# Perceiver block on one core: latents and projection of the queries for two pairs in every second round, keys' rows by transposes, scores in two halves

## The chip, the cores and the metric

One core of one Trainium2 chip runs the whole program. The metric is device microseconds of one execution; the profile beside it is of one execution of its own, and all times in it count from the start of its span. TensorE is PE in the views, its weight loads PEld, VectorE is DVE, ScalarE is ACT, GpSimd is POOL, and SyncE (SP) issues the DMAs.

## The reference

There are 32 examples of 64 query tokens and 128 context tokens, 512 features each, all float32. Three residual blocks follow each other.

```python
# cross attention, 16 heads, latents of 32 (keys) and 64 (queries)
C_q = Q @ Wq_d ; C_kv = K @ Wkv_d            # Q = layernorm(x), K = ctx
CqWqk = (C_q @ W_qk).reshape(b, n, H, LKV)
scores = einsum('bnhl,bkl->bhnk', CqWqk, C_kv) / sqrt(LKV) ; attn = softmax(scores)
out = einsum('bhnk,bkhd->bnhd', attn, (C_kv @ Wv_u).reshape(b, nkv, H, HD))
# one-head self attention of width 128 on layernorm(x), with biases
# feed forward on layernorm(x): x @ hadamard, rows rounded to 4 bits, times ternary weights
```

## The kernel before, in words

Two examples make a pair: 128 query rows, 256 context rows; there are 16 pairs. All engines walk through rounds i = -1 to 17. Round i works on four pairs at once: `front` computes latents, projection and scores of pair i+1, `cross` the softmax and pooled values of pair i, `self_` the second attention of pair i-1, `quant` the feed forward of pair i-2. Rounds 4 to 11 are a hardware loop over two rounds (`par` = 0, then 1); the others are written out. The order in each engine's body is fixed by the code, and semaphores (`made`: written by TensorE, `read`: copied out of PSUM, `done`: by DVE, ACT or POOL) tie the engines. TensorE's queue is in order, so a wait in it holds up all behind it.

The steps that matter here, by lines of TensorE's body: L608 values of pair i-1 through Wv; L615 transposes of x3; L624 latents of the queries (weights 64 columns wide, two column halves of the array, each summing two chunks of features); L630 latents of the context (32 columns, four column strips); L644 Hadamard product; L649, L600, L683, L687 transposes and the q, k, v products of the second attention; L695 transposes of the rounded rows; L712 q times k; L656 projection of the query latents for all 16 heads (the two partial sums of L624 lie in 128 partitions, and `wqk2` holds W_qk twice, so the product adds them); L659 the context latents repeated in four strips (`ckv`, columns 0 to 255); L662 the same latents with the keys on partitions (`fold`, 32 columns each); L733 pooled values in latent space; L740 transpose of the second attention's probabilities p2; L753 ternary product (int); L758 o2t; L768 scores of the next pair, 32 products with 32 rows and 64 columns of weights, into banks 0 to 3; L778 output product of the second attention. A float32 product has two matmul records, a transpose one. PSUM has 8 banks: 0 to 3 for scores and transposed probabilities, B1 to B4 for all others.

ScalarE copies what TensorE made, between its exponentials: x3t, lat, x2t, prob_t, q_t, p2t, u_t, o2t. VectorE takes the maxima of the scores (L417), makes x3 (L540), sums, statistics and the rounding.

## Time and profile before

| | |
|---|---|
| median of 3 runs | 337.03 us (336.73 to 337.52) |
| the profiled execution, its own time | 338.82 us |
| its span | 337.0 us |
| TensorE busy | 318.1 us, 94% |
| VectorE, ScalarE, GpSimd busy | 239.7, 211.1, 88.2 us |
| mean share of the DMA engines in a round | 0.20 |

The profile has a page, and the trace behind it answers queries. In order of time a row gives start, duration, engine, line, what is written from what, how many records, and in brackets how long the engine had been idle and who ended it. The records of a matmul overlap, so that the start of the next row less the start of a row, not its duration, is what a step takes of TensorE's time.

### The profile page before, as it was taken

The numbers are of one execution on the slowest core, as the hardware profiler recorded it, in microseconds if no ns is written. First come the engines' busy times: TensorE is split into PE (matmuls) and PEld (weight loads), VectorE is DVE, ScalarE is ACT, GpSimd is POOL, SyncE is SP. The second block draws the span as 40 slices with busy tenths as digits, with TensorE's granted clock in tenths as the row PEclk, the third lists the DMA queues.
The fourth block names the chain that finished last, engine by engine and source line by source line (L and its number), as shares of the span: only waits on it lengthen the run. The fifth ranks groups of instructions, "written<-read, shape, count | busy, mean of one in ns | idle before, by whom it ended". The sixth has DMA issues, their size and how long they took to land.

```text
span 337.0 us, 8519 instructions
## 1 busy us (share of the span) xinstructions
PE 318.1 (94%) x3204; PEld 231.7 (69%) x3204; DVE 239.7 (71%) x517; ACT 211.1 (63%) x565; POOL 88.2 (26%) x129
## 2 busy tenths in 40 slices
PE   8897899999999999999999999999999999898995
PEld 6775666758595867768585857677685858575754
DVE  1489638686877868686868768686868778686435
ACT  2474858577586758586685867585866757673210
POOL 2000533131332323231223313232312223131320
PEclk9997999999999999999999999999999999999999
DMA  7891203040211303040402103030402020000000
GB/s 227 277 375 59 97 3 124 2 158 0 103 58 38 122 33 124 5 151 0 155 0 94 62 31 124 31 124 5 151 2 65 0 66 0 33 3 31 2 31 31
DMA packets 13481, 25.25 MB, mean 75 GB/s; under 512 B 3216, under 2 KB 3984, under 8 KB 13456
## 3 DMA queue, kind: packets, MB, share of 16 engines
q1 hardware_dynamic: 13456, 24.91, 21.0%
q8 instruction: 16, 0.26, 0.3%
q14 instruction: 9, 0.07, 0.1%
HBM read 20.71 MB, written 4.19 MB: 74 GB/s over the span
## 4 chain that ended last, share of the span: by engine, by line
PE 75%; DVE 15%; DMA 3%; ACT 2%; issue 2%; SPq 2%; DVEq 0%
PE ps L644 17%; PE ps L683 9%; PE ps L600 7%; DVE mx L417 6%; PE ps L768 5%; PE ps L733 5%; PE ps L656 5%; PE ps L687 4%; PE ps L753 4%; DVE x L540 3%; DMA w_rows<-weight 3%; PE ps L615 3%; PE ps L624 2%; PE ps L630 2%; PE ps L649 2%
## 5 line engine op out<-in xcount | busy, mean ns | idle before, releaser
L301 ACT ACTIVATE prob<-ps,nmx,qk_scale 128x128 f32<-128x128 f32 x256 | 95.9, 463 | 56.3 <-DVE nmx L421 56.3
L644 PE MATMUL ps<-had_s,x3t 128*128 128x512 f32 x128 | 59.2, 605 | 1.2 <-ACT x3t L295 1.2
L417 DVE TENSOR_REDUCE mx<-ps 128x8 f32<-128x1024 f32 x32 | 39.0, 1218 | 13.3 <-PE ps L768 13.3
L644 PEld LDWEIGHTS ps<-had_s,x3t 128*128 128x128 f32 x128 | 23.0, 189 | 30.1 <-issue 24.6
L426 DVE TENSOR_REDUCE sum_a<-prob 128x8 f32<-128x1024 f32 x32 | 37.5, 1209 | 2.3 <-ACT prob L301 2.3
L295 ACT ACTIVATE prob_t<-ps 128x512 f32<-128x512 f32 x64 | 35.1, 612 | 5.6 <-PE ps L600 5.5
L600 PE MATMUL ps<-ident,prob 128*128 128x128 f32 x256 | 33.3, 273 | 1.0 <-ACT prob L301 1.0
L288 POOL TENSOR_TENSOR res<-prod,x 128x512 f32<-128x512 f32 x15 | 19.0, 1267 | 57.0 <-DVE prod L530 57.0
L683 PE MATMUL ps<-x2t,wqkv_s 128*128 128x128 f32 x256 | 32.5, 280 | 0.8 <-ACT x2t L295 0.8
L683 PEld LDWEIGHTS ps<-x2t,wqkv_s 128*128 128x128 f32 x256 | 29.8, 191 | 2.0 <-ACT x2t L295 1.2
L284 POOL TENSOR_TENSOR qk_scale<-aux,power 128x1 f32<-128x1 f32 x16 | 8.8, 548 | 83.1 <-DVE aux L496 83.1
L600 PEld LDWEIGHTS ps<-ident,prob 128*128 128x128 f32 x256 | 28.3, 141 | 1.7 <-ACT prob L301 1.5
L262 POOL TENSOR_TENSOR rstd<-aux,power 128x1 f32<-128x1 f32 x16 | 8.8, 548 | 69.7 <-DVE aux L446 69.7
L530 DVE SCALAR_TENSOR_TENSOR prod<-ps,qscale,scale_row 128x512 f32<-128x512 f32 x15 | 11.3, 751 | 19.0 <-PE ps L753 19.0
L608 PEld LDWEIGHTS ps<-wv_bd,u_t 128*128 128x128 f32 x128 | 17.3, 197 | 7.2 <-issue 7.2
L279 POOL TENSOR_TENSOR x2b<-x,const_row 128x512 f32<-128x512 f32 x16 | 20.3, 1270 | 0.1
L768 PE MATMUL ps<-ckv,q_t 32*64 32x128 f32 x1024 | 19.3, 278 | 0.1
L656 PE MATMUL ps<-lat,wqk 128*128 128x128 f32 x128 | 18.4, 287 | 0.2 <-ACT lat L295 0.2
L778 PE MATMUL ps<-wo_s,o2t 128*128 128x512 f32 x32 | 18.0, 645 | 0.5 <-ACT o2t L295 0.4
L733 PE MATMUL ps<-prob_t,ckv 128*32 128x256 f32 x256 | 17.1, 383 | 0.9 <-ACT prob_t L295 0.5
L608 PE MATMUL ps<-wv_bd,u_t 128*128 128x128 f32 x128 | 17.6, 282 | 0.0
L768 PEld LDWEIGHTS ps<-ckv,q_t 32*64 32x64 f32 x1024 | 15.5, 130 | 2.4 <-issue 0.7
(114 smaller groups left out, 566.0 us busy)
## 6 DMA issues: line engine op xcount, KB each, us to landing
ct<-ctx_cols SPq DMA_DIRECT2D x16, 512.0 KB, 3.7
xt<-x_cols SPq DMA_DIRECT2D x16, 256.0 KB, 2.6
xr<-x_rows SPq DMA_DIRECT2D x16, 256.0 KB, 3.8
y<-res SPq DMA_DIRECT2D x15, 256.0 KB, 2.0
w_rows<-weight SPq DMA_DIRECT2D x1, 1024.0 KB, 10.5
had_s<-hadamard SPq DMA_DIRECT2D x1, 1024.0 KB, 8.6
wqkv_s<-wqkv SPq DMA_DIRECT2D x1, 768.0 KB, 10.2
wqk<-w_qk SPq DMA_DIRECT2D x2, 128.0 KB, 4.1
```

Source lines behind the costliest of these rows:

```text
L279: nc.gpsimd.tensor_tensor(x2b[:], x2[:], const_row[:], ALU.add).then_inc(done["x2b"], 1)
L295: return nc.scalar.activation(dst, src, ACT.Copy)
L301: last = nc.scalar.activation(prob[:, h, :], ps[:, h // 4, (h % 4) * P:(h % 4) * P + P], ACT.Exp, bias=nmx[:, h:h + 1], scale=qk_scale[:])
L417: V.tensor_reduce(mx[:, h], ps[:, 2 * half:2 * half + 2, :].rearrange("p r (c k) -> p (r c) k", c=EC), AX.X, ALU.max).then_inc(done["mx"], 1)
L426: V.tensor_reduce(sum_a[:, h], prob[:, h, :], AX.X, ALU.add).then_inc(done["sum"], 1)
L600: mm = pe.transpose(ps[:, r, c * P:(c + 1) * P], prob[:, 4 * r + c, :], ident[:])
L608: mm = pe.matmul(ps[:, B1, c * P:(c + 1) * P], u_t[:, c, :], wv_bd[:, c, :], start=True, stop=True)
L644: mm = pe.matmul(ps[:, B4, :], x3t[:, c, :], had_s[:, c, :], start=(c == 0), stop=(c == EC - 1))
L656: mm = pe.matmul(ps[:, B2, c * P:(c + 1) * P], wqk2[:, c * P:(c + 1) * P], lat[:, 0:P], start=True, stop=True)
L683: mm = pe.matmul(ps[:, B1, s * P:(s + 1) * P], wqkv_s[:, c, s * P:(s + 1) * P], x2t[:, c, :], start=(c == 0), stop=(c == EC - 1))
L733: mm = pe.matmul(ps[32 * r:32 * r + 32, B2, :].rearrange("p (c t) -> p c t", c=EC) [:, :, 64 * bb:64 * bb + 64], ckv[:, par, 2 * SKV + LAT ...
L768: mm = pe.matmul(ps[64 * bb:64 * bb + 64, r, c * P:(c + 1) * P], q_t[g, bb, c, :], ckv[g, 1 - par, bb * SKV:(bb + 1) * SKV], start=True, s ...
```

## The change

The latents of the queries and their projection are made for two pairs at once, in the odd rounds (`par == 1`); even rounds have neither, but for rounds -1 and 0, which do one pair each as before (`alone`). In an odd round the query latents come right behind L608's step: the two column halves of the array take a pair each, all four chunks of features are summed in place, so `lat` holds pair i+1 in partitions 0 to 63 and pair i+2 in 64 to 127. The projection then multiplies 64 rows of each, alternating between the halves of partitions, into bank 0 and bank 1, behind the v product; ScalarE copies the two banks to two slots of `q_t`. Even rounds copy only the context's columns of `lat`.

The keys' rows are no longer products with `fold`: at the next round's head two transposes of `ckv` go to bank B3, and ScalarE copies 32 columns of each to `ckv_k`. The latents move from B3 to B2, x3's transposes from B2 to B4. The transpose of p2 comes behind the int product, and the scores are cut in two halves, one ahead of o2t and one behind it. On VectorE the maximum of the second attention moves ahead of the row statistics of the next pair. SyncE loads x for two pairs in odd rounds.

```diff
         lat = sb("lat", [P, P + 2 * SKV])
-        q_t = sb("q_t", [P, 2, EC, SQ])
-        ckv = sb("ckv", [P, 2, 2 * SKV + 2 * LAT])
+        q_t = sb("q_t", [P, 2, 2, EC, SQ])
+        ckv = sb("ckv", [P, 2, 2 * SKV])
+        ckv_k = sb("ckv_k", [P, 2, LAT])
...
         def _(sp):
-            def load_cols(pair, par):
-                after(sp, made["lat"], pair - 2)
+            def load_queries(pair, par):
                 sp.dma_start(xt[:, par], x_cols[bass.ds(pair, 1)].rearrange("o p c t -> (o p) c t")).then_inc(ld_xt[par], 16)
+            def load_context(pair, par):
...
             sp.dma_start(wqkv_s[:], wqkv.rearrange("(c p) n -> p c n", p=P)).then_inc(ld_w["wqkv"], 16)
-            load_cols(2, 0)
+            sp.wait_ge(made["lat"], 1)
+            load_queries(2, 0)
+            load_context(2, 0)
...
                 if not pre or 0 <= i < PAIRS - 3:
-                    load_cols(i + 3, 1 - par)
+                    after(sp, made["lat"], i + 1)
+                    if pre and i == 0:
+                        load_queries(i + 3, 1)
+                    elif par == 1:
+                        load_queries(i + 3, 0)
+                        if not pre or i + 4 < PAIRS:
+                            load_queries(i + 4, 1)
+                    load_context(i + 3, 1 - par)
...
+                def q_copy(slot, bank):
+                    copy(q_t[:, slot], ps[:, bank, :].rearrange("p (c b q) -> p b c q", c=EC, b=2)).then_inc(read["qt"], 1)
...
                     after(act, made["had"], i - 3)
-                    copy(x3t[:], ps[:, B2, :].rearrange("p (c t) -> p c t", c=EC)).then_inc(read["x3t"], 1)
+                    copy(x3t[:], ps[:, B4, :].rearrange("p (c t) -> p c t", c=EC)).then_inc(read["x3t"], 1)
...
                     after(act, made["lat"], i + 1)
-                    copy(lat[:], ps[:, B3, 0:P + 2 * SKV]).then_inc(read["lat"], 1)
+                    cols = slice(0 if alone(i) or par == 1 else P, P + 2 * SKV)
+                    copy(lat[:, cols], ps[:, B2, cols]).then_inc(read["lat"], 1)
+                if cross:
+                    after(act, made["ckvk"], i)
+                    after(act, made["u"], i - 1)
+                    copy(ckv_k[:], ps[:, B3, 0:2 * P].rearrange("p (b l) -> p b l", b=2)[:, :, 0:LAT])\
+                        .then_inc(read["ckvk"], 1)
...
                     copy(v2[:], ps[:, B2, 0:P]).then_inc(read["v"], 1)
+                if front and par == 1 and not alone(i):
+                    act.wait_ge(made["qt"], k + 3)
+                    q_copy(0, 0)
...
                     pt_copy(3)
-                if front:
+                if front and alone(i):
                     after(act, made["qt"], i + 1)
-                    copy(q_t[:], ps[:, B2, :].rearrange("p (c b q) -> p b c q", c=EC, b=2)).then_inc(read["qt"], 1)
+                    q_copy(1 - par, query_bank(i))
+                elif front and par == 1:
+                    q_copy(1, 1)
...
                     after(act, made["ckv"], i + 1)
-                    copy(ckv[:, 1 - par], ps[:, B1, 0:2 * SKV + 2 * LAT]).then_inc(read["ckv"], 1)
+                    copy(ckv[:, 1 - par], ps[:, B1, 0:2 * SKV]).then_inc(read["ckv"], 1)
...
                         .then_inc(read["qit"], 1)
+                if self_:
+                    after(dve, made["s2"], i - 1)
+                    V.tensor_reduce(mx2[:], ps[:, B3, 0:SQ], AX.X, ALU.max).then_inc(done["mx2"], 1)
+                    after(dve, done["mx2"], i - 1)
+                    V.tensor_scalar(nmx2[:], mx2[:], -float(D2) ** -0.5, None, ALU.mult).then_inc(done["nmx2"], 1)
...
                     mm.then_inc(made["xo"], 1)
+                if front and alone(i):
+                    pe.wait_ge(ld_xt[1 - par], 16)
+                    for h in range(2):
+                        for t in range(2):
+                            c = 2 * t + h
+                            pe.matmul(ps[64 * t:64 * t + 64, B2, 0:P], wq_c[:, c, :], xt[:, 1 - par, c, :],
+                                      start=(h == 0), stop=(h == 1))
+                elif front and par == 1:
+                    for t in range(2):
+                        pe.wait_ge(ld_xt[t], (k + 2) * 16)
+                    for c in range(EC):
+                        for t in range(2):
+                            pe.matmul(ps[64 * t:64 * t + 64, B2, 0:P], wq_c[:, c, :], xt[:, t, c, :],
+                                      start=(c == 0), stop=(c == EC - 1))
...
                     after(pe, read["wo"], i - 2)
-                    for c in range(EC):
-                        mm = pe.transpose(ps[:, B2, c * P:(c + 1) * P], x3[:, par, c * P:(c + 1) * P], ident[:])
+                    after(pe, read["int"], i - 3)
+                    if first and i == 2:
+                        pe.wait_ge(row_read, 1)
+                    for c in range(EC):
+                        mm = pe.transpose(ps[:, B4, c * P:(c + 1) * P], x3[:, par, c * P:(c + 1) * P], ident[:])
...
                 if front:
-                    if first and i == 1:
-                        pe.wait_ge(ternt_read, 2)
-                    pe.wait_ge(ld_xt[1 - par], (k + par + 1) * 16)
-                    for h in range(2):
-                        for t in range(2):
-                            c = 2 * t + h
-                            pe.matmul(ps[64 * t:64 * t + 64, B3, 0:P], wq_c[:, c, :], xt[:, 1 - par, c, :],
-                                      start=(h == 0), stop=(h == 1))
...
                     for c in range(EC):
-                        mm = pe.matmul(ps[32 * c:32 * c + 32, B3, P:P + 2 * SKV], wkv_s[:, c, :], ct[:, 1 - par, c, :],
+                        mm = pe.matmul(ps[32 * c:32 * c + 32, B2, P:P + 2 * SKV], wkv_s[:, c, :], ct[:, 1 - par, c, :],
...
                     mm.then_inc(made["lat"], 1)
+                if cross:
+                    after(pe, read["ckv"], i)
+                    if quant:
+                        after(pe, read["wo"], i - 2)
+                    if first and i == 1:
+                        pe.wait_ge(ternt_read, 2)
+                    for bb in range(2):
+                        mm = pe.transpose(ps[:, B3, bb * P:(bb + 1) * P], ckv[:, par, bb * SKV:(bb + 1) * SKV], ident[:])
+                    mm.then_inc(made["ckvk"], 1)
...
                     after(pe, read["x3t"], i - 2)
-                    after(pe, read["int"], i - 3)
                     if first and i == 2:
-                        pe.wait_ge(row_read, 1)
...
                     after(pe, done["x2n"], i - 1)
+                    if front:
+                        after(pe, read["lat"], i + 1)
...
                     mm.then_inc(made["x2t"], 1)
+                def scores(half):
+                    for c in (2 * half, 2 * half + 1):
+                        for r in range(4):
+                            g = slice(32 * r, 32 * r + 32)
+                            for bb in range(2):
+                                mm = pe.matmul(ps[64 * bb:64 * bb + 64, r, c * P:(c + 1) * P], q_t[g, 1 - par, bb, c, :],
+                                               ckv[g, 1 - par, bb * SKV:(bb + 1) * SKV], start=True, stop=True)
+                    return mm
...
                         pe.wait_ge(fold_made, 2)
-                    for c in range(EC):
-                        mm = pe.matmul(ps[:, B2, c * P:(c + 1) * P], wqk2[:, c * P:(c + 1) * P], lat[:, 0:P],
-                                       start=True, stop=True)
-                    mm.then_inc(made["qt"], 1)
+                    if alone(i):
+                        for c in range(EC):
+                            mm = pe.matmul(ps[:, query_bank(i), c * P:(c + 1) * P], wqk2[:, c * P:(c + 1) * P], lat[:, 0:P],
+                                           start=True, stop=True)
+                        mm.then_inc(made["qt"], 1)
                     pe.matmul(ps[:, B1, 0:2 * SKV], fold4[:].rearrange("p r l -> p (r l)"), lat[:, P:P + 2 * SKV],
-                              start=True, stop=True)
-                    for bb in range(2):
-                        mm = pe.matmul(ps[:, B1, 2 * SKV + LAT * bb:2 * SKV + LAT * (bb + 1)],
-                                       lat[:, P + SKV * bb:P + SKV * (bb + 1)], fold[:], start=True, stop=True)
-                    mm.then_inc(made["ckv"], 1)
+                              start=True, stop=True).then_inc(made["ckv"], 1)
...
                     mm.then_inc(made["v"], 1)
+                if front and par == 1 and not alone(i):
+                    pe.wait_ge(read["pt"], i * 4 + 2)
+                    for c in range(EC):
+                        for t in range(2):
+                            g = slice(64 * t, 64 * t + 64)
+                            mm = pe.matmul(ps[:, t, c * P:(c + 1) * P], wqk2[g, c * P:(c + 1) * P], lat[g, 0:P],
+                                           start=True, stop=True)
+                    mm.then_inc(made["qt"], 1)
...
                     after(pe, read["qk"], i - 1)
-                    if front:
-                        after(pe, read["lat"], i + 1)
+                    if cross:
+                        after(pe, read["ckvk"], i)
...
                     after(pe, read["lat"], i + 1)
-                    if self_:
-                        after(pe, read["v"], i - 1)
...
                     if first and i == -1:
-                        keep_busy(2, 0)
+                        keep_busy(2, B3)
...
                     pe.wait_ge(read["pt"], i * 4 + 4)
-                    if front:
-                        after(pe, read["qt"], i + 1)
-                    elif self_:
+                    after(pe, read["ckvk"], i)
+                    if first and i == 0:
+                        pe.wait_ge(read["qt"], 2)
+                    if self_:
...
                                            [:, :, 64 * bb:64 * bb + 64],
-                                           ckv[:, par, 2 * SKV + LAT * bb:2 * SKV + LAT * (bb + 1)],
+                                           ckv_k[:, bb, :],
...
                     mm.then_inc(made["u"], 1)
-                if self_:
-                    after(pe, done["exp2"], i - 1, 2)
-                    pe.transpose(ps[:, B3, 0:P], p2[:], ident[:]).then_inc(made["p2t"], 1)
...
                 if self_:
+                    after(pe, done["exp2"], i - 1, 2)
+                    pe.transpose(ps[:, B3, 0:P], p2[:], ident[:]).then_inc(made["p2t"], 1)
+                if front:
+                    if alone(i):
+                        after(pe, read["qt"], i + 1)
+                    elif par == 1:
+                        pe.wait_ge(read["qt"], 2 * k + 4)
+                    after(pe, read["ckv"], i + 1)
+                    if cross:
+                        pe.wait_ge(read["pt"], i * 4 + 4)
+                    scores(0)
+                if self_:
...
                 if front:
-                    after(pe, read["qt"], i + 1)
-                    after(pe, read["ckv"], i + 1)
-                    if cross:
-                        pe.wait_ge(read["pt"], i * 4 + 4)
-                    for c in range(EC):
-                        for r in range(4):
-                            g = slice(32 * r, 32 * r + 32)
-                            for bb in range(2):
-                                mm = pe.matmul(ps[64 * bb:64 * bb + 64, r, c * P:(c + 1) * P], q_t[g, bb, c, :],
-                                               ckv[g, 1 - par, bb * SKV:(bb + 1) * SKV], start=True, stop=True)
-                    mm.then_inc(made["s"], 1)
+                    scores(1).then_inc(made["s"], 1)
```

The order of TensorE's instructions in the second round of the loop body (the odd one) at its head, before and then of the change; L608 and L641 are the same step, as are L615 and L665, L630 and L672, L644 and L693.

```order
L608 MATMUL ps<-wv_bd,u_t 128x128 x4
L615 MATMUL ps<-ident,x 128x128 x4
L620 ISA
L624 MATMUL ps<-xt,wq_c 64x128 x4
L630 MATMUL ps<-ct,wkv_s 32x256 x4
L644 MATMUL ps<-had_s,x3t 128x512 x4
```

```order
L641 MATMUL ps<-wv_bd,u_t 128x128 x4
L652 ISA
L655 MATMUL ps<-xt,wq_c 64x128 x8
L665 MATMUL ps<-ident,x 128x128 x4
L672 MATMUL ps<-ct,wkv_s 32x256 x4
L682 MATMUL ps<-ident,ckv 128x128 x2
L693 MATMUL ps<-had_s,x3t 128x512 x4
```

The query latents have moved ahead of x3's transposes, eight products instead of four, and two transposes of ckv stand ahead of the Hadamard product. The even round has the same rows without L652 and L655.

The order of TensorE's instructions at the end of the same round, from q times k on, before and then of the change; L656 and L752 are the projection, L733 and L797 the pooled values, L768 and L707 the scores.

```order
L712 MATMUL ps<-k,q 64x64 x2
L656 MATMUL ps<-lat,wqk 128x128 x4
L659 MATMUL ps<-lat,fold 128x256
L662 MATMUL ps<-fold,lat 128x32 x2
L726 ISA
L733 MATMUL ps<-prob_t,ckv 32x4x64 x8
L740 MATMUL ps<-ident,p 128x128
L753 MATMUL ps<-tern_t,qi_t 128x512 x4
L758 MATMUL ps<-p2t,v 128x128
L768 MATMUL ps<-ckv,q_t 64x128 x32
L778 MATMUL ps<-wo_s,o2t 128x512
```

```order
L777 MATMUL ps<-k,q 64x64 x2
L720 MATMUL ps<-lat,fold 128x256
L789 REGISTER_ALU
L797 MATMUL ps<-prob_t,ckv_k 32x4x64 x8
L814 MATMUL ps<-tern_t,qi_t 128x512 x4
L818 MATMUL ps<-ident,p 128x128
L823 REGISTER_ALU
L707 MATMUL ps<-ckv,q_t 64x128 x16
L831 MATMUL ps<-p2t,v 128x128
L707 MATMUL ps<-ckv,q_t 64x128 x16
L841 MATMUL ps<-wo_s,o2t 128x512
```

The products with `fold` of 32 columns are gone, the projection has left this place, the int product is ahead of the transpose of p2, and o2t stands between the halves of the scores.

The projection's new place, in TensorE's order of the change, odd round, between the v product and the transposes of the rounded rows:

```order
L740 MATMUL ps<-x2t,wqkv_s 128x128 x8
L744 MATMUL ps<-wqkv_s,x2t 128x128 x4
L748 ISA
L752 MATMUL ps<-lat,wqk 128x128 x8
L760 MATMUL ps<-ident_b,qi 128x128 x4
```

Before, these rows stood there without L748 and L752.

## Rows read from the trace of the kernel before

**Rows 1.** The page, part 1: busy time, share of the span, instructions.

```profile
PE 318.1 (94%) x3204; PEld 231.7 (69%) x3204; DVE 239.7 (71%) x517; ACT 211.1 (63%) x565; POOL 88.2 (26%) x129
```

**Rows 2.** Whom TensorE waited for: us in total, times, longest.

```profile
PE ps L615 <- DVE x L540: 5.7, 15, 0.8
...
PE ps L649 <- POOL x2n L265: 0.6, 1, 0.6
```

**Rows 3.** Busy time of each engine in one round, clock, DMA share, GB/s.

```profile
162.10:180.68 18.58, 18.25 (x192) 13.23 (x192) 14.40 (x32) 13.03 (x37) 5.16 (x7) 1.00 0.20 69
```

**Rows 4.** TensorE in order of time, one round of the loop.

```profile
171.67 1.04 PE L600 MATMUL ps<-ident,prob 128*128 128x128 f32 x8
172.64 0.34 PE L712 MATMUL ps<-k,q 128*64 128x64 f32 x4
172.91 1.16 PE L656 MATMUL ps<-lat,wqk 128*128 128x128 f32 x8
173.90 0.60 PE L659 MATMUL ps<-lat,fold 128*128 128x256 f32 x2
174.34 0.53 PE L662 MATMUL ps<-fold,lat 128*128 128x32 f32 x4
174.84 1.07 PE L733 MATMUL ps<-prob_t,ckv 128*32 128x256 f32 x16
175.84 0.33 PE L740 MATMUL ps<-ident,p 128*128 128x128 f32 x1
176.01 1.03 PE L753 MATMUL ps<-tern_t,qi_t 128*128 128x512 bf16 x4
176.87 0.38 PE L758 MATMUL ps<-p2t,v 128*128 128x128 f32 x2
177.19 1.21 PE L768 MATMUL ps<-ckv,q_t 32*64 32x128 f32 x64
178.32 1.12 PE L778 MATMUL ps<-wo_s,o2t 128*128 128x512 f32 x2
179.29 1.05 PE L608 MATMUL ps<-wv_bd,u_t 128*128 128x128 f32 x8
180.68 0.66 PE L615 MATMUL ps<-ident,x 128*128 128x128 f32 x4 [0.33 <-DVE x L540]
181.26 0.66 PE L624 MATMUL ps<-xt,wq_c 128*64 128x128 f32 x8
181.85 0.64 PE L630 MATMUL ps<-ct,wkv_s 128*32 128x256 f32 x8
182.42 3.70 PE L644 MATMUL ps<-had_s,x3t 128*128 128x512 f32 x8
```

**Rows 5.** All engines in order of time, the next round; rows of DVE, ACT, PE.

```profile
179.87 0.75 DVE L540 SCALAR_TENSOR_TENSOR x<-ps,rsum,x2b 128x512 f32<-128x512 f32 x1
...
181.37 0.60 ACT L295 ACTIVATE x3t<-ps 128x512 f32<-128x512 f32 x1
...
190.89 1.09 ACT L295 ACTIVATE prob_t<-ps 128x512 f32<-128x512 f32 x2 [0.39 <-PE ps L600]
...
193.18 0.30 ACT L354 ACTIVATE p<-ps,nmx 64x64 f32<-64x64 f32 x1
...
194.43 0.33 PE L740 MATMUL ps<-ident,p 128*128 128x128 f32 x1
...
194.79 0.28 ACT L295 ACTIVATE p2t<-ps 128x128 f32<-128x128 f32 x1 [0.34 <-PE ps L740]
...
195.45 0.38 PE L758 MATMUL ps<-p2t,v 128*128 128x128 f32 x2
...
195.87 0.28 ACT L295 ACTIVATE o2t<-ps 128x128 f32<-128x128 f32 x1 [0.32 <-PE ps L758]
```

**Rows 6.** TensorE in order of time, round 15.

```profile
304.82 0.33 PE L740 MATMUL ps<-ident,p 128*128 128x128 f32 x1
...
306.60 1.13 PE L778 MATMUL ps<-wo_s,o2t 128*128 128x512 f32 x2 [0.37 <-ACT o2t L295]
```

**Rows 7.** TensorE in order of time, end of round 0.

```profile
26.97 1.05 PE L589 MATMUL ps<-ident_b,tern 128*128 128x128 bf16 x16 [2.08 <-DVE const_row L454]
```

21 lines of the change are left out of this document (11 added, 10 removed).

## The prediction

> **What bounds the kernel now.** I read the page's first part, then who TensorE waited for, then one round of the loop in order of time on TensorE, then the same round on the other engines, last the ends of the program. TensorE is busy 94% of the span [rows 1]. A round of the loop takes 18.58 us, TensorE is busy 18.25 of it, at a granted clock of 1.00 [rows 3]. The rest is one wait: L615, the transposes of x3, waits 0.33 us for DVE's x3 in each round (5.7 us in 15 rounds, the longest item of its waits) [rows 2, 4]. VectorE (14.40) and ScalarE (13.03) have 4 and 5 us to spare per round [rows 3]. So a microsecond of TensorE's time taken from a round is a microsecond of the kernel, as long as the copies on ScalarE between two of its steps still arrive in time. The reader should see in [rows 4] that the next start less this start is the price of a step, and that this price has two parts: a full-array record of 128 columns costs 0.11 us (L600: 8 in 0.97, which at a change of shape holds 0.1 more), however few columns it streams (L662: 4 records of 32 columns in 0.50); and where the shape of the weights changes, the step before pays about 0.1 us more (L758: 2 records in 0.32). Steps in narrow tiles overlap: L768 has 64 records in 1.13 us, over 4 row strips times 2 column halves, 8 records per tile; L624 has 4 per tile in 0.59 [rows 4]. From these two a block of narrow tiles costs 0.59 for 4 records per tile and 1.0 to 1.1 for 8.
>
> **The change, part by part, in us of TensorE's time.** Even rounds project nothing; odd rounds do two pairs.
> (A) L656, L659, L662 filled 172.91 to 174.84, 1.93 us [rows 4]. L656 leaves this place and L662 goes. What stays is one product of two 256-column records before a change of shape; the nearest step is L630 with two 256-column records per tile, 0.57 [rows 4]; its weights are narrower, so I add half a 0.11 us record: 0.62. Each round: -1.31.
> (B) L624 goes: -0.59 [rows 4].
> (C) Two transposes of ckv are put ahead of the Hadamard product: 2 x 0.11, less a weight load that is now hidden under them: +0.19.
> (D) The end of the round, L733 to L778, took 174.84 to 178.32, 3.48 us [rows 4]. The int product is now ahead of the transpose of p2, and the scores stand in two halves around o2t. New: pooled values 1.03, int product 0.86 + 0.05 (first weight load bare), transpose 0.11 + 0.1 (before a tiled step), half the scores 0.62 (4 records per tile: between L624's 0.59 and 0.65), o2t 0.42 (L758's 0.32 and a bare weight load), half the scores 0.62; together 3.82: +0.34. If the split were free it would be 0; if each half cost what the whole costs, +1.4. I take the rate by records per tile.
> (E) Odd rounds: the latents of two pairs, 8 records per tile, stand between L608's step and x3's transposes: 1.02, and the change of shape 0.2. L608 start to L615 start was 1.39 with the 0.33 wait in it [rows 4]; now 0.98 + 1.02 = 2.00, and x3 (179.87 + 0.75 [rows 5]) is there long before: +0.61.
> (F) Odd rounds: the projection of two pairs in 16 records, K = 64 each, into two banks. No row shows a 64-row strip. If the two strips overlap as L768's four do, it is 8 records per strip at 0.11, entry 0.2, exit 0.2, a bare load 0.1 and 0.05 behind it, less what the neighbour gave up: +1.23. If the strips do not overlap, 16 x 0.11 + 0.35 = 2.1. I take 1.23, since L768 proves overlap between row strips: without it 64 records over two column halves would be 32 x 0.11 = 3.5 us, not 1.13.
> Even round: -1.31 - 0.59 + 0.19 + 0.34 = -1.37. Odd round: the same + 0.61 + 1.23 = +0.47.
>
> **Who could be late.** Measured from the step that each waits for: x3t's copy starts 0.69 after L615 (181.37 against 180.68) and takes 0.60, so the Hadamard product may start at 1.34; its turn comes at 0.58 + 0.57 + 0.22 = 1.37 now, 1.74 before [rows 4, 5]. Tight, no wait. The last prob_t copies end at 191.98, 0.76 behind the start of q.k at 191.22 (172.64 a round earlier [rows 4]); the pooled values' turn is now at 0.27 + 0.62 = 0.89. Tight too. Softmax 2's exponentials (193.18) no longer sit behind the q_t copy: DVE's maximum is moved ahead of the row statistics, and they are done 1 us before the transpose needs them. Behind that maximum on DVE are only the row statistics of the next pair, needed 3 us later. p2t is copied 0.36 after L740's start, for 0.28 [rows 5]; the first half of the scores covers 0.8. o2t's copy ends 0.70 behind L758's start (195.87 + 0.28 against 195.45), behind u_t's on ScalarE; its cover is 0.42 + 0.62. In odd rounds the first q_t copy fits between v's and prob_t's. The ckv_k copy (some 0.25) falls into ScalarE's wait for DVE's second nmx. If a cover fails, each costs 0.1 to 0.3 per round, 1.5 to 4 us in all. The x loads for two pairs are issued two rounds ahead; with DMA at 0.20 [rows 3] and landings of a few us that is hidden.
>
> **The ends.** At the start nothing is won: the ternary weights' transposes wait 2.08 for DVE [rows 7], and in round 1 TensorE waits 0.6 for x2n [rows 2], which swallows the longer latents. Round 1 itself gives 0.3. Rounds 15 and 16 have no scores to cover the p2t copy: from L740 to L778 took 1.78 [rows 6]; now 0.91 (int) + 0.31 + 0.28 + 0.05 (copy, laid bare) + 0.53 + 0.28 + 0.05 = 2.41, so +0.63 each, +1.3 together.
>
> **Sum.** Rounds 2 to 13 are six even and six odd: 6 x (-0.90) = -5.4; round 14 (even) -1.4; round 1 -0.3; the end +1.3. Together -5.8. The profiled execution took 338.82 (span 337.0), so 333.0; the median of the runs is 337.03, 1.8 below it, so **331.2**.
>
> **A rule weighed.** L662's 32-column records cost 0.11 to 0.125 us each [rows 4]. The Trainium skill (TensorEngine Tiling (Array Packing), Instruction Overhead) says that a matmul has about 60 cycles of overhead, so that fewer columns than that save nothing; by it the four records would cost about 0.1 us together, and removing them would give 6 us less than I count over 16 rounds. The trace decides: 0.50.
>
> **Rivals.**
> (1) The strips take turns in (F) because a strip cannot load weights while it streams: 2.1 instead of 1.23 in 7 rounds, +6.1, 337.3: no change. For it: no 64-row row exists. Against: L768's records, 8 per tile in 1.13, leave 0.11 per record and no room for a bare 64-column load each. The Trainium skill (TensorE: Matmul & The Clock Gate, The mechanism) says that a weight load overlaps with a running matmul only where the row group differs; by that rule this rival is the forecast, but full-array records come here every 0.11 us, each with a weight load of its own [rows 4], so the trace disagrees. Chance 0.08.
> (2) Slower: the strips write all 128 columns of the array, and each record waits for the other strip's end, as at a change of shape (0.2 instead of 0.11): 16 x 0.2 + 0.35 = 3.5, +16 us in 7 rounds, 347. The point is 2.06 per projection: above it the change loses. Chance 0.06.
> (3) The covers fail: o2t's or p2t's copy, or x3t's and prob_t's, stalls TensorE 0.1 to 0.3 in most rounds: 332.7 to 335.5. For it: four margins of 0.03 to 0.3. Against: each is worked out from copies that are in the rows. Chance 0.18.
> (4) The change of shapes costs less than I take it for, and (D) is near zero: -0.3 x 13, 327.5 to 329.5. Chance 0.08.
> (5) The forecast, 329.5 to 332.7: chance 0.60.
>
> **Numbers.** The range 329.3 to 335.0 holds (5), most of (3) and some of (4). 0.2% (0.7 us) is about what a measurement of this kernel tells from no change: faster 0.86, same 0.07, slower 0.07.
>
> **What the profile after would show.** Odd and even rounds of about 19.05 and 17.2 us in turn. The projection as 16 records of 64*128 in 1.1 us, not 2; the two halves of the scores 0.62 each; the 0.33 wait for x3 only in even rounds; TensorE's waits for x3t, prob_t, p2t, o2t still near zero in the loop, and 0.3 to 0.4 at p2t in rounds 15 and 16. Wrong would be: projection records 0.1 us apart, or a new wait of over 0.1 us per round on one of the four copies.

## The result, and the profile after

| | before | the change |
|---|---|---|
| median of the runs made side by side | 337.27 us (336.73 to 337.85, 4 runs) | 331.31 us (331.07 to 331.48, 4 runs) |
| ratio | | 0.9823, 95% interval 0.9803 to 0.9842 |
| the profiled execution, its own time; span | 338.82; 337.0 us | 331.07; 329.3 us |

The change is faster by 6.0 us, 0.1 from the forecast of 331.2. That total hides two errors that nearly cancel (rounds 2 to 14 gained 0.4 us less than forecast, the end lost 0.4 less), so that the last tenth is luck; and the experiments found an order of the same work that is about 5 us better still.

The page of the change, part 1, answers to [rows 1]: TensorE is still the engine that is nearly always busy, with 6.9 us less work.

```profile
PE 311.2 (95%) x3157; PEld 216.7 (66%) x3172; DVE 239.8 (73%) x517; ACT 210.6 (64%) x581; POOL 88.3 (27%) x129
```

Whom TensorE waited for in the change (us in total, times, longest); it answers to [rows 2]. The wait for x3 is left in 9 rounds of the 15, and its sum fell from 5.7 to 4.0. The row with "issue" is not a wait: of the four records of L814 the first is missing in the trace, so that the gap ahead of the other three looks idle.

```profile
PE ps L665 <- DVE x L573: 4.0, 9, 0.6
PE ps L814 <- issue: 2.2, 14, 0.2
...
PE ps L740 <- ACT x2t L314: 0.8, 2, 0.5
PE ps L831 <- ACT p2t L314: 0.7, 2, 0.4
```

Two rounds of the loop in the windows view, the even one and then the odd one (span, then busy time of PE, PEld, DVE, ACT, POOL, granted clock, DMA share, GB/s); they answer to [rows 3]. Both together take 36.50 us, where two rounds of before take 2 x 18.58 = 37.16.

```profile
155.13:172.68 17.55, 16.91 (x181) 11.30 (x174) 14.35 (x31) 12.34 (x35) 5.08 (x8) 1.00 0.18 60
172.68:191.63 18.95, 18.79 (x212) 13.10 (x205) 14.49 (x31) 13.52 (x37) 5.25 (x8) 1.00 0.27 83
```

TensorE in order of time over these two rounds; it answers to [rows 4]. L841 opens a round.

```profile
155.13 1.12 PE L841 MATMUL ps<-wo_s,o2t 128*128 128x512 f32 x2
...
157.63 0.65 PE L665 MATMUL ps<-ident,x 128*128 128x128 f32 x4 [0.48 <-DVE x L573]
158.21 0.64 PE L672 MATMUL ps<-ct,wkv_s 128*32 128x256 f32 x8
...
159.06 3.69 PE L693 MATMUL ps<-had_s,x3t 128*128 128x512 f32 x8
...
163.02 1.04 PE L633 MATMUL ps<-ident,prob 128*128 128x128 f32 x8
164.06 2.05 PE L740 MATMUL ps<-x2t,wqkv_s 128*128 128x128 f32 x16
...
168.31 0.70 PE L720 MATMUL ps<-lat,fold 128*128 128x256 f32 x2
168.94 1.07 PE L797 MATMUL ps<-prob_t,ckv_k 128*32 128x256 f32 x16
170.16 0.81 PE L814 MATMUL ps<-tern_t,qi_t 128*128 128x512 bf16 x3 [0.16 <-issue]
...
171.01 0.69 PE L707 MATMUL ps<-ckv,q_t 32*64 32x128 f32 x32
171.64 0.49 PE L831 MATMUL ps<-p2t,v 128*128 128x128 f32 x2
172.06 0.69 PE L707 MATMUL ps<-ckv,q_t 32*64 32x128 f32 x32
172.68 1.13 PE L841 MATMUL ps<-wo_s,o2t 128*128 128x512 f32 x2
...
174.62 1.09 PE L655 MATMUL ps<-xt,wq_c 128*64 128x128 f32 x16
175.65 0.66 PE L665 MATMUL ps<-ident,x 128*128 128x128 f32 x4
...
180.97 1.04 PE L633 MATMUL ps<-ident,prob 128*128 128x128 f32 x8
181.84 2.03 PE L740 MATMUL ps<-x2t,wqkv_s 128*128 128x128 f32 x16
183.71 1.06 PE L744 MATMUL ps<-wqkv_s,x2t 128*128 128x128 f32 x8
184.70 1.16 PE L752 MATMUL ps<-lat,wqk 64*128 64x128 f32 x16
185.79 0.40 PE L760 MATMUL ps<-ident_b,qi 128*128 128x128 bf16 x4
```

Start to next start gives the prices: the products with `fold4` 168.94 - 168.31 = 0.63; the latents of two pairs 1.03; the projection of two pairs 185.79 - 184.70 = 1.09; a half of the scores 0.63 (171.64 - 171.01), o2t between them 0.42.

### The profile page after: what moved, and what is told of

It is laid out like the page before. It is cut to its first block, busy times and chain, and to the rows that moved or that the text cites. A ratio compares the mean times of both kernels' runs of the same rounds, so it can differ in the third digit from the quotient of the medians.

```text
span 329.3 us, 8506 instructions
## 1 busy us (share of the span) xinstructions
PE 311.2 (95%) x3157; PEld 216.7 (66%) x3172; DVE 239.8 (73%) x517; ACT 210.6 (64%) x581; POOL 88.3 (27%) x129
## 4 chain that ended last, share of the span: by engine, by line
PE 79%; DVE 11%; DMA 3%; issue 2%; ACT 2%; SPq 2%; DVEq 0%
PE ps L693 17%; PE ps L740 9%; PE ps L633 8%; PE ps L707 6%; PE ps L797 5%; PE ps L744 4%; PE ps L814 4%; DVE mx L450 4%; PE ps L665 3%; PE ps L720 3%; PE ps L841 3%; DMA w_rows<-weight 3%; PE ps L752 2%; PE ps L672 2%; PE ps L831 2%
## 5 line engine op out<-in xcount | busy, mean ns | idle before, releaser
L693 PE MATMUL ps<-had_s,x3t 128*128 128x512 f32 x128 | 58.4, 599 | 0.9 <-ACT x3t L314 0.9
L693 PEld LDWEIGHTS ps<-had_s,x3t 128*128 128x128 f32 x128 | 23.0, 189 | 24.8 <-issue 23.0
L633 PE MATMUL ps<-ident,prob 128*128 128x128 f32 x256 | 33.4, 274 | 0.8 <-ACT prob L320 0.8
L740 PE MATMUL ps<-x2t,wqkv_s 128*128 128x128 f32 x256 | 32.7, 281 | 0.8 <-ACT x2t L314 0.8
L740 PEld LDWEIGHTS ps<-x2t,wqkv_s 128*128 128x128 f32 x256 | 29.8, 191 | 2.9 <-ACT x2t L314 2.2
L633 PEld LDWEIGHTS ps<-ident,prob 128*128 128x128 f32 x256 | 28.2, 141 | 2.0 <-ACT prob L320 1.8
L707 PE MATMUL ps<-ckv,q_t 32*64 32x128 f32 x1024 | 21.8, 280 | 0.2 <-ACT ckv L314 0.2
L641 PEld LDWEIGHTS ps<-wv_bd,u_t 128*128 128x128 f32 x128 | 16.7, 192 | 7.2 <-issue 7.2
L707 PEld LDWEIGHTS ps<-ckv,q_t 32*64 32x64 f32 x1024 | 14.6, 131 | 6.1 <-issue 4.0
L841 PE MATMUL ps<-wo_s,o2t 128*128 128x512 f32 x32 | 18.0, 645 | 0.5 <-ACT o2t L314 0.4
L797 PE MATMUL ps<-prob_t,ckv_k 128*32 128x256 f32 x256 | 17.1, 385 | 1.0 <-ACT q_t L314 0.5
L582 PE MATMUL ps<-mean_w 128*128 128x128 f32 x102 | 15.8, 298 | 1.4 <-POOL p L261 1.4
L641 PE MATMUL ps<-wv_bd,u_t 128*128 128x128 f32 x128 | 16.9, 275 | 0.0
```

What stands on the lines that cost most here:

```text
L633: mm = pe.transpose(ps[:, r, c * P:(c + 1) * P], prob[:, 4 * r + c, :], ident[:])
L641: mm = pe.matmul(ps[:, B1, c * P:(c + 1) * P], u_t[:, c, :], wv_bd[:, c, :], start=True, stop=True)
L693: mm = pe.matmul(ps[:, B4, :], x3t[:, c, :], had_s[:, c, :], start=(c == 0), stop=(c == EC - 1))
L707: mm = pe.matmul(ps[64 * bb:64 * bb + 64, r, c * P:(c + 1) * P], q_t[g, 1 - par, bb, c, :], ckv[g, 1 - par, bb * SKV:(bb + 1) * SKV], star ...
L740: mm = pe.matmul(ps[:, B1, s * P:(s + 1) * P], wqkv_s[:, c, s * P:(s + 1) * P], x2t[:, c, :], start=(c == 0), stop=(c == EC - 1))
L797: mm = pe.matmul(ps[32 * r:32 * r + 32, B2, :].rearrange("p (c t) -> p c t", c=EC) [:, :, 64 * bb:64 * bb + 64], ckv_k[:, bb, :], prob_t[: ...
```

## The experiments

Beside the experiments the kernel before was measured again on three chips, with medians of 337.99, 338.04 and 337.85 where it had 337.27 beside the change, so kernels are compared by their ratio to it, and a difference of ratios is turned into us with 338. "Even, odd" are loop rounds from output product to output product; the change has 17.54 and 18.95 to 18.96.

| kernel | median us | ratio, 95% interval | even, odd |
|---|---|---|---|
| the change | 331.31 | 0.9823, 0.9803 to 0.9842 | 17.54, 18.95 |
| e1_strip_order | 335.14 | 0.9926, 0.9897 to 0.9955 | 17.55, 19.50 |
| e2_scores_whole | 335.72 | 0.9932, 0.9911 to 0.9953 | 17.80, 19.29 |
| e4_keys_by_products | 337.38 | 0.9987, 0.9968 to 1.0006 | 17.91, 19.32 |
| e5_one_pair | 341.28 | 1.0102, 1.0069 to 1.0134 | 18.95, 18.73 |
| e9_one_pair_bank0 | 333.55 | 0.9864, 0.9838 to 0.9889 | 18.44, 18.21 |
| e3_old_end | 327.49 | 0.9684, 0.9662 to 0.9705 | 17.26, 18.79 |
| e6_unrolled | 330.41 | 0.9769, 0.9746 to 0.9792 | 17.34, 18.96 |
| e7_old_end_copy_late | 327.0 | 0.9668, 0.9646 to 0.9690 | 17.26, 18.69 |
| e8_old_end_unrolled | 326.17 | 0.9651, 0.9625 to 0.9677 | 17.02, 18.69 |
| e10_old_end_max_late | 335.72 | 0.9939, 0.9916 to 0.9962 | 18.34, 18.90 |
| e11_max_late | 334.38 | 0.9893, 0.9867 to 0.9919 | 18.01, 18.96 |

**The order of the strips.** The projection does one half of the partitions first and then the other.

```diff
-                    for c in range(EC):
-                        for t in range(2):
+                    for t in range(2):
+                        for c in range(EC):
                             g = slice(64 * t, 64 * t + 64)
```

> The changed kernel with one edit: the 16 records of the projection in odd rounds go through all four column groups of the first 64-row strip, then all four of the second, instead of alternating. Theory: the strips overlap only where neighbouring records go to different strips, so the block takes 16 x 0.11 + 0.25 = 2.0 us instead of 1.09; +0.9 in 7 rounds, +6.3 us, about 337.6. Rival: TensorE's queue looks far enough ahead to overlap the strips in any order, 331.3 unchanged. The price of the first rival of the prediction (strips take turns) is thereby measured too.

TensorE in order of time, the projection in an odd round of this kernel:

```profile
187.01 1.71 PE L752 MATMUL ps<-lat,wqk 64*128 64x128 f32 x16
188.66 0.40 PE L760 MATMUL ps<-ident_b,qi 128*128 128x128 bf16 x4
```

The block takes 1.65 us, against 1.09, and the odd round 0.55 more; 7 such rounds are 3.85 us, and the ratios differ by 1.0% (3.5 us). So neither theory had it. Taken one by one, the records of a strip start 0.112 us apart in either order, from its second record on. Alternated, the records of the two strips start in pairs, 0.006 apart. In sequence the second strip's first record starts at 187.57, just behind the fifth of the first strip's eight, so that only the last three of the first strip run beside the second: most of the overlap is lost, but not all. The two strips also write two banks, 0 and 1, in both orders; which of the two differences lets them overlap, rows or banks, no run separates.

**Scores in one piece behind o2t**, the transpose of p2 still behind the int product.

```diff
+                if self_:
+                    after(pe, read["p2t"], i - 1)
+                    after(pe, read["v"], i - 1)
+                    pe.matmul(ps[:, B3, 0:P], v2[:], p2t[:], start=True, stop=True).then_inc(made["o2t"], 1)
                 if front:
...
                     scores(0)
-                if self_:
-                    after(pe, read["p2t"], i - 1)
-                    after(pe, read["v"], i - 1)
-                    pe.matmul(ps[:, B3, 0:P], v2[:], p2t[:], start=True, stop=True).then_inc(made["o2t"], 1)
-                if front:
                     scores(1).then_inc(made["s"], 1)
```

> The changed kernel with one edit: all scores stand behind o2t in one block, as before, the transpose of p2 stays behind the int product. Theory: the first half of the scores covers the p2t copy, which is laid bare now: from the transpose's start 0.27 + 0.04 + 0.28 + 0.05 = 0.64 to o2t, 0.42 for o2t, 1.14 for the scores, 2.2 us against 1.87 now; +0.33 in 14 rounds, +4.6 us, about 336. Rival: the split costs more (two changes of shape) than it covers, and undoing it gives 0.1 to 0.2 per round, 328.5 to 330.

TensorE in this kernel, the end of a round:

```profile
175.90 0.49 PE L822 MATMUL ps<-p2t,v 128*128 128x128 f32 x2 [0.37 <-ACT p2t L314]
```

The theory held: the copy of p2t is laid bare in every round, 0.37 us, as in rounds 15 and 16 of the change, and an odd round is 0.34 longer, an even one 0.26. (With the scores in one piece VectorE's maximum starts 0.11 behind the start of the output product, with two halves 0.18, and only the even round, which waits for x3, gains by that.) The split pays once the transpose stands where it does. Whether the transpose should stand there is the next question but one.

**The keys' rows by products with `fold` again**, 32 columns each, and the transposes of ckv and the ckv_k copy gone.

```diff
-                    for bb in range(2):
-                        mm = pe.transpose(ps[:, B3, bb * P:(bb + 1) * P], ckv[:, par, bb * SKV:(bb + 1) * SKV], ident[:])
-                    mm.then_inc(made["ckvk"], 1)
...
+                    for bb in range(2):
+                        mm = pe.matmul(ps[:, B1, 2 * SKV + LAT * bb:2 * SKV + LAT * (bb + 1)],
+                                       lat[:, P + SKV * bb:P + SKV * (bb + 1)], fold[:], start=True, stop=True)
```

> The changed kernel with the keys' rows made as before, by two 32-column products with fold behind the repeated latents; the two transposes of ckv and the copy ckv_k are gone. Theory: the products cost 0.31 to 0.4 per round (L659 to L733 took 0.94 before, the same place takes 0.63 now), and taking the transposes (0.28) out from ahead of the Hadamard product gives nothing back, since x3t's copy ends there at the same moment: +0.31 to 0.4 in 15 rounds, 336 to 337.3. Rival: the transposes cost their own 0.28 of TensorE's time, so undoing is worth 0.03 to 0.1 per round: 331.8 to 332.8.

TensorE in this kernel: the head of the round, and the products' place.

```profile
162.97 0.64 PE L667 MATMUL ps<-ct,wkv_s 128*32 128x256 f32 x8
163.80 3.70 PE L679 MATMUL ps<-had_s,x3t 128*128 128x512 f32 x8 [0.20 <-ACT x3t L314]
...
173.07 0.70 PE L706 MATMUL ps<-lat,fold 128*128 128x256 f32 x2
...
174.06 1.07 PE L788 MATMUL ps<-prob_t,ckv 128*32 128x256 f32 x16
```

The transposes are nearly free: where they stood, TensorE now waits 0.20 for x3t. L672 to L693 was 0.85 in the change and L667 to L679 is 0.83 here, so that removing them gives 0.02 back, while the block at L706 costs 0.99 instead of 0.63. 0.36 in each of 15 rounds is 5.4 us, the ratios differ by 1.64%, 5.5 us. Without this part nearly the whole gain is gone; what it would be worth by itself, with the other parts undone, no run shows.

**One pair per round.** Latents and projection of one pair in each round, as in the kernel before, with the rest of the change kept; the projection goes to bank B2.

```diff
         def alone(i):
-            return isinstance(i, int) and i <= 0
+            return True
...
+                    if front:
+                        after(pe, read["qt"], i + 1)
```

> The changed kernel with latents and projection of one pair in every round, the latents still ahead of x3's transposes and in the new banks, keys by transposes and scores in halves kept. Theory: even rounds gain the projection's 0.89, the latents' 0.59 lie in the place of the 0.48 wait for x3 and take the 0.17 wait for x2t away: +0.76; odd rounds lose 1.18 (paired projection), 0.44 (second pair's latents) and gain 0.89: -0.73. Together about 0, 331 to 333: pairing itself is worth next to nothing against one pair a round at the new place. Rival: pairing is where the gain is; 1.78 - 1.18 = 0.6 per two rounds and more lost again, 335.5 or above.

Whom TensorE waited for in this kernel, the first row; and one such wait in order of time:

```profile
PE ps L794 <- ACT q_t L309: 6.9, 15, 0.5
```

```profile
155.21 1.16 PE L712 MATMUL ps<-lat,wqk 128*128 128x128 f32 x8
156.21 0.60 PE L715 MATMUL ps<-lat,fold 128*128 128x256 f32 x2
157.25 1.07 PE L794 MATMUL ps<-prob_t,ckv_k 128*32 128x256 f32 x16 [0.45 <-ACT q_t L309]
```

This missed by 8 to 10 us, and the miss teaches more than the hits. The pooled values write the bank that the q_t copy reads. In the kernel before L659 and L662 covered this copy for 0.94 us [rows 4]; with L662 gone only 0.59 is left, and each round waits 0.45. The wait makes 6.9 us of the miss. To test that, the same kernel with the projection in bank 0, which the pooled values don't write:

```diff
                     if alone(i):
+                        if self_:
+                            pe.wait_ge(read["pt"], i * 4 + 1)
                         for c in range(EC):
```

> As the kernel with one pair a round, but the projection is written to bank 0 (free once the first prob_t copy is done) instead of B2, so that the pooled values, which overwrite B2, no longer wait for the q_t copy. In the run before that wait took 0.45 us in each of 15 rounds, 6.9 us, and was not in my sum. Theory: without it a pair of rounds takes 36.8 to 36.9 against 36.5, so about +2.5 us on the change, 333 to 335: most of what pairing is worth is this wait, not TensorE's work. Rival: TensorE's work for one pair a round is itself worth more than 1 us per two rounds, and this is still at 338 or above.

The wait is gone, the ratio is 0.9864, and its two rounds take 18.44 + 18.21 = 36.65 us, where the change takes 36.50. So in the loop two pairs at once are in themselves worth 0.15 us per two rounds. Over the whole kernel the ratios differ by 0.4%, 1.4 us, with intervals that just overlap; by the two profiles 1.5 us of the change's lead arise in rounds 12 to 14. What pairs bought was mainly room: banks 0 and 1 for the projection, away from the tight copy. Bank 0 alone buys nearly the same.

**The kernel before once more**, for its start.

> The kernel before, looked at once more, for its start. In the profile of before the ternary weights' transposes (L589) start at 26.97 us, in that of the change at 25.28, while the medians differ by 6.0 and the spans by 7.7. Theory: the weight matrix landed late by chance (10.5 us against 8.5), and this look at before shows L589 at 25 to 26 or another value again. Rival: the change's start is 1.7 us shorter by its own doing, and before shows 26.9 again.

```profile
27.78 1.07 PE L589 MATMUL ps<-ident_b,tern 128*128 128x128 bf16 x16
```

This row is that of [rows 7]: 27.78 here, 26.97 there, and L622, the same step, at 25.28 in the change. The loop's rounds are the same 18.58 in both executions of before. The step started at another moment again, but not because of the weight matrix: w_rows landed in 8.0 us here and 10.5 there, and the 2.08 us wait of [rows 7] is absent; TensorE was later all along (the scores of round 0, L768, at 26.64 against 23.69). In the eight experiments that leave the change's start as it is, L622 starts at 24.79 to 27.96 and the transposes of x2n in round 1 at 33.77 to 36.43; in the two executions of before these stand at 35.95 and 36.17, in the change at 34.00. So the start moves by 2.7 to 3.2 us between executions, for a reason that stays open, and the 1.95 us by which the change's profile leads at that step is not shown to be the change's doing. It is why the spans differ by 7.7 us where the rest of the program accounts for 5.75.

The profile of before has one more thing at its start. TensorE stood idle for 2.08 us up to 26.97, and its granted clock was 0.56 from 28 to 29 us, 0.50 from 29 to 31 and 0.73 from 31 to 32: for most of this time it ran at 1.2 GHz instead of 2.4, and L608's step took 1.75 us where it takes about 1.0 in the loop. The other execution of before had no such idle time there and a clock of 1.00 in the same stretches; yet the two reach the output product of round 1 at 48.10 and 48.32, since x2n ends a wait in both (0.62 and 0.89 us) that takes most of it up.

**The order of before at the round's end**: transpose of p2, int product, o2t, scores in one piece.

```diff
                     mm.then_inc(made["u"], 1)
+                if self_:
+                    after(pe, done["exp2"], i - 1, 2)
+                    pe.transpose(ps[:, B3, 0:P], p2[:], ident[:]).then_inc(made["p2t"], 1)
                 if quant:
...
                 if self_:
-                    after(pe, done["exp2"], i - 1, 2)
-                    pe.transpose(ps[:, B3, 0:P], p2[:], ident[:]).then_inc(made["p2t"], 1)
+                    after(pe, read["p2t"], i - 1)
+                    after(pe, read["v"], i - 1)
+                    pe.matmul(ps[:, B3, 0:P], v2[:], p2t[:], start=True, stop=True).then_inc(made["o2t"], 1)
...
```

The step of o2t between the halves of the scores goes, as in e2_scores_whole.

> The changed kernel with the end of the round in the order of before: transpose of p2, int product, o2t, all scores in one block. Theory: the order of before took 3.48 us from the pooled values on, the new one takes 3.74, and p2's exponentials are done 0.1 us before their new turn in even rounds and 0.1 to 0.15 behind it in odd ones: -0.26 in 7 even rounds, -0.13 in 7 odd ones, -2.7 us and the 0.6 of rounds 15 and 16: about 328. Rival: without the projection and the fold products between q.k and the pooled values the exponentials are late by more than 0.3 us per round, and the new order was needed: 331 or above.

The median is 327.49 for a forecast of about 328, and the ratio falls to 0.9684, 4.7 us under the change. So the new order of the end is a loss that the rest of the change pays for. In a second step the second q_t copy of odd rounds goes behind the exponentials of the second attention and the ckv copy on ScalarE:

```diff
-                elif front and par == 1:
-                    q_copy(1, 1)
...
                     copy(ckv[:, 1 - par], ps[:, B1, 0:2 * SKV]).then_inc(read["ckv"], 1)
+                    if par == 1 and not alone(i):
+                        q_copy(1, 1)
```

> As the kernel with the old end of the round, and ScalarE's second q_t copy of odd rounds moved behind p2's exponentials and the ckv copy. Theory: it takes 0.6 us out of the way of the exponentials, so odd rounds gain the full 0.26 as well; it is 0.9 us less than the run before, about 327.2. Rival: the copy is then late for the scores, and it is not faster than the run before.

TensorE at the end of a round of this kernel:

```profile
168.53 1.07 PE L797 MATMUL ps<-prob_t,ckv_k 128*32 128x256 f32 x16
169.58 0.33 PE L804 MATMUL ps<-ident,p 128*128 128x128 f32 x1
...
170.61 0.39 PE L822 MATMUL ps<-p2t,v 128*128 128x128 f32 x2
170.92 1.21 PE L707 MATMUL ps<-ckv,q_t 32*64 32x128 f32 x64
172.06 1.13 PE L840 MATMUL ps<-wo_s,o2t 128*128 128x512 f32 x2
```

From the pooled values to the output product it takes 172.06 - 168.53 = 3.53 us, the change 3.74; the int product again covers the p2t copy, the scores in one piece the o2t copy, and the odd round is 0.1 shorter than in e3_old_end, though the medians of the two don't differ by more than their intervals.

**The maximum of the second attention late.** VectorE takes it behind the row statistics again, as in the kernel before, first in e7 and then in the change itself.

```diff
-                if self_:
-                    after(dve, made["s2"], i - 1)
-                    V.tensor_reduce(mx2[:], ps[:, B3, 0:SQ], AX.X, ALU.max).then_inc(done["mx2"], 1)
...
                     V.tensor_scalar(aux1[:], mv1[:, 1:2], EPS, float(LAT), ALU.add, ALU.mult).then_inc(done["aux1"], 1)
+                if self_:
+                    after(dve, made["s2"], i - 1)
+                    V.tensor_reduce(mx2[:], ps[:, B3, 0:SQ], AX.X, ALU.max).then_inc(done["mx2"], 1)
...
```

> As the kernel with the old end and the late copy, with VectorE's maximum of the second attention behind the row statistics of the next pair again, as in the kernel before. Theory: in even rounds the exponentials of p2 come 1.0 to 1.1 us later (0.68 + 0.2 + 0.2 of statistics), and the transpose of p2, which has no slack there, waits as long: +0.9 in 7 even rounds, nothing in odd ones, where the statistics are done before q.k: about 333.5 where that kernel is 327. Rival: the order on VectorE is free, 327.

> The changed kernel with one edit, VectorE's maximum of the second attention behind the row statistics again. Theory: the exponentials are done 0.7 us before their turn now, and would be 0.4 late in even rounds: +0.4 x 7 = +2.8, about 334. Rival: the new place of the transpose, behind the int product, has slack enough, 331.3 unchanged; then the move on VectorE buys nothing in the change as it stands.

All engines in order of time in e10_old_end_max_late, the rows of the second attention:

```profile
170.73 0.34 PE L777 MATMUL ps<-k,q 128*64 128x64 f32 x4
...
172.43 0.22 DVE L532 TENSOR_REDUCE mx<-ps 128x1 f32<-128x64 f32 x1
...
173.75 0.33 PE L804 MATMUL ps<-ident,p 128*128 128x128 f32 x1 [1.05 <-ACT p L385]
```

The first kernel missed its forecast of 333.5 by 2 us: its even rounds are 1.08 longer than in e7_old_end_copy_late, for 0.9, and its odd rounds 0.21, for nothing. The second came out as forecast. The scores of the second attention are there at 171.07 (170.73 + 0.34), VectorE comes to them at 172.43, and TensorE waits 1.05. The two lines on VectorE are worth 9 us with the old end (0.9668 against 0.9939) and 2.4 us in the change (0.9823 against 0.9893), where the int product ahead of the transpose covers part of the lateness. In the kernel before, the projection and the products with `fold` stood between these scores and the transpose: L712 to L740 took 3.20 us [rows 4], L777 to L804 takes 1.97 here without the wait. So the transpose of p2 had two remedies in the change, an earlier maximum and a later place, and needed only the first.

**The rounds written out.** `LOOP = (2, 6)` becomes `(2, 3)`: the loop body runs once, the other rounds stand in the program.

> The changed kernel with rounds 6 to 11 written out (the hardware loop runs once, over rounds 4 and 5). Theory: even rounds in the loop take 17.54 to 17.68 us and 17.25 to 17.34 where they are written out, since VectorE's and ScalarE's chain from the scores to x2t, which bounds them now, waits 0.3 longer in the loop for registers and the branch; odd rounds do not care. -0.27 x 3 = -0.8, 330.5. Rival: the written-out rounds of the profile are shorter for another reason (less DMA, the ends), or the longer program loads its code late: 331.3 or more.

The median is 330.41, 0.9 us under the change, and the ratio 0.9769, which makes it 1.8; the rows give 0.9: even rounds take 17.34, in the loop 17.54 and in its first pass 17.68, and odd ones don't change. The one even round that is still in the loop's body takes 17.34 too; with a single pass the body has no register instructions left (VectorE's queue holds 16 FUSED_REGOPS and 48 ALU_OP in the change, none and 1 here). With the old end and the late copy:

> As the kernel with the old end and the late copy, with rounds 6 to 11 written out. Theory: its even rounds take 17.25 to 17.63 us in the loop and 16.91 to 17.01 outside, so writing three of them out and shortening the one in the loop gives 3 x 0.25 + 0.4 = 1.1 us: about 326 where the kernel with the loop is 327. Rival: the two gains share the same wait and do not add: 327.

326.17 us (325.8 to 327.02), ratio 0.9651: the best kernel of this study, by the ratios 5.8 us under the change and 11.8 under before. Its interval overlaps that of e7_old_end_copy_late, but its even rounds are 0.24 shorter.

## Why the prediction was right, step by step

**What bounds the kernel** held: TensorE's time by starts accounts for nearly every difference. The rounds were forecast at 17.2 and 19.05 and take 17.54 and 18.95; two of them gain 0.66, not 0.90.

**(A), (B), (E), (F)** held within 0.05: (A) 0.63 for 0.62; (E) L841 to L665 in the odd round 175.65 - 172.68 = 2.97 against 2.36 [rows 4], +0.61 exactly; (F) 185.79 - 183.71 = 2.08 against 0.90 before for the same neighbour, +1.18 for +1.23.

**(C)** was mis-sized: from L672 to L693 it takes 0.85 and 0.84 against 0.57 before [rows 4], +0.27 to 0.28 for +0.19. Only in the odd round does the Hadamard product give 0.09 of it back (180.53 - 177.08 = 3.45 against 3.54). And e4_keys_by_products shows what the price is: the transposes stand in a time part of which would be a wait for x3t.

**(D)** was 3.74 for 3.82, +0.26 for +0.34: right, and a cost, as the experiments confirm. What the prediction did not ask is whether the cost is needed.

**Who could be late** held for the four copies that it names: x3t, prob_t, p2t and o2t have no wait in the loop. It missed the even round of the loop. These are rows of VectorE and ScalarE there in the change:

```profile
155.31 1.23 DVE L450 TENSOR_REDUCE mx<-ps 128x8 f32<-128x1024 f32 x1 [1.09 <-PE ps L707]
...
158.29 0.69 DVE L470 TENSOR_TENSOR x<-xm,xr 128x512 f32<-128x512 f32 x1 [0.19 <-DVE xm L464]
...
161.41 0.57 DVE L454 TENSOR_SCALAR nmx<-mx,qk_scale 128x8 f32<-128x8 f32 x1
162.02 1.50 ACT L320 ACTIVATE prob<-ps,nmx,qk_scale 128x128 f32<-128x128 f32 x4 [1.25 <-DVE nmx L454]
163.41 0.61 ACT L314 ACTIVATE x2t<-ps 128x512 f32<-128x512 f32 x1
```

And these of the kernel before, the even round that opens the window of [rows 3]:

```profile
159.85 1.22 DVE L417 TENSOR_REDUCE mx<-ps 128x8 f32<-128x1024 f32 x1 [0.61 <-PE ps L768]
...
162.83 0.69 DVE L437 TENSOR_TENSOR x<-xm,xr 128x512 f32<-128x512 f32 x1 [0.19 <-DVE xm L431]
...
165.95 0.57 DVE L421 TENSOR_SCALAR nmx<-mx,qk_scale 128x8 f32<-128x8 f32 x1
```

From the start of the maximum to x3's transposes it takes 157.63 - 155.31 = 2.32 us in the change and 162.10 - 159.85 = 2.25 before, and the maximum starts 0.18 behind the start of the output product where it was 0.11. In an even round TensorE has nothing else to do ahead of x3's transposes, so the wait was taken as the 0.33 of before and is 0.48. VectorE's own part is as long as ever, 2.19 in both. The 0.07 at the maximum is the price of the split scores (e2 and e3, with the scores in one piece, have 0.11 again); why TensorE starts 0.13 behind the end of x3, and not 0.06, stays open.

Then the second nmx ends at 161.98, the exponentials hold ScalarE, and the x2t copy ends at 164.02, so that L740 starts 1.04 behind L633, not 0.87 as in the odd round. The forecast's list of what could be late has no x2t in it. With 0.15 at x3, 0.17 at x2t and 0.09 in (C), less 0.08 in (D), the even round is 0.33 over its forecast.

The prediction worked out both kinds of round from one stretch of before [rows 4], the end of an even round and the head of an odd one, which was fair there, since all rounds of that loop take 18.58. In the kernel before, VectorE had the small gap ahead of L437 and the nmx of 0.57 already, under a TensorE that came later. e6_unrolled shows which part belongs to the loop: written out, nmx takes 0.36, L740 starts 0.88 behind L633 and L693's step takes 3.45, which makes up the 0.20; the wait for x3 stays at 0.50. Why VectorE is slower in the loop stays open.

**The ends.** TensorE of the change in round 15:

```profile
297.06 0.27 PE L818 MATMUL ps<-ident,p 128*128 128x128 f32 x1
297.70 0.49 PE L831 MATMUL ps<-p2t,v 128*128 128x128 f32 x2 [0.37 <-ACT p2t L314]
298.55 1.13 PE L841 MATMUL ps<-wo_s,o2t 128*128 128x512 f32 x2 [0.37 <-ACT o2t L314]
```

The waits are where they were forecast. Round 15 lost 0.66 (forecast 0.63), round 16 0.35 (forecast 0.63). The forecast took round 15's price for both. In round 16 of before, the transpose of p2 stood behind ten products that only keep TensorE busy (L549):

```profile
318.60 1.38 PE L549 MATMUL ps<-mean_w 128*128 128x128 f32 x10
320.05 0.33 PE L740 MATMUL ps<-ident,p 128*128 128x128 f32 x1
```

The last of the ten starts at 319.71, and at 0.11 each the transpose's turn was at 319.82, but the exponentials of p2 ended at 319.99, so it lost 0.23 there. In the change the int product stands in that place and covers this wait.

In sum: -0.3 in round 1 (from x2n's transposes to those of x3 in round 2: 14.22 us against 14.53 before); -6.4 in rounds 2 to 14 (235.97 us from L665 to L665, 242.34 from L615 to L615 before) for a forecast of -6.8; +0.9 behind them for +1.3. That is -5.8, as forecast, and the medians say -6.0. In rounds 2 to 14 the four even loop rounds each gain 0.34 less than forecast, 1.4 us together. Of that 0.5 came back in the odd rounds up to 11, 0.1 each, mostly by (D), and 0.6 in round 13, which takes 18.95 like the other odd ones but 19.06 in the kernel before: the prediction had taken 18.58 for all.

**The rivals.** (1) and (2), turns of the strips, fell with 1.09. The trace shows 16 records of 64 rows in that time. The Trainium skill (TensorE: Matmul & The Clock Gate, The mechanism) says in its list that a weight load overlaps only with a matmul of another row group, though a sentence above it names a background weight buffer as well. The alternated strips are no test of that rule, since each load may run beside the other strip's matmul. Full-array records, which all have the same rows, are one: they come every 0.12 us (L740: 16 from 181.84 to 183.71) with as many loads as records, and a record of 512 columns takes 0.43 (L693: 8 from 177.08 to 180.53), so that by estimate 128 columns stream for 0.11 and leave no time for a load by itself. So the trace disagrees with the rule; and so do the records of one strip in e1_strip_order, 0.112 apart. (3), failing covers, holds in small: 0.17 us in even rounds at x2t, by a chain of VectorE that it didn't name. (4), the scores split for nothing, fell: 0.26.

## What to carry to other kernels

When a block of work is taken off the bounding engine, list what it covered: here L656 and L662 covered a copy of q_t and a late maximum, and the place of two lines on VectorE was worth 9 us. When several edits each guard against the same lateness, undo them one by one, since the later ones may only cost. Model every kind of round (even, odd, in the loop, written out) from its own rows.

## What the runs showed of the hardware

Two 64-row strips of float32 products, alternated between strips and banks, finish 16 records in 1.09 us; one strip after the other takes 1.65. Within a strip the records are 0.112 us apart both times. The two halves of the scores take 0.63 each, the whole 1.14, so cutting it costs 0.12, and the full-array step between them 0.1 more (0.42 for 0.31); behind a wait (e2_scores_whole) that step takes 0.42 as well. The even round's body is 0.20 us longer in the hardware loop than written out (0.24 with the old end), the odd one not at all (18.96 both ways). Executions of kernels with the same start are up to 2.7 us apart at x2n's transposes of round 1.
